# A four-layer kernel: distances of one batch made among the softmax tiles of another in the last attention, two slots for the row norms, split loads in the first feed-forward

## What is computed

```python
    x = x + _layernorm(_L3_attn_ref(_layernorm(x, axis=-1), ...), axis=-1)
```

```python
        scores = jnp.einsum('bid,bjd->bij', q, k) / jnp.sqrt(...)
        qp = _linear(hidden_states, Wtq, btq)
        diff = qp[:, :, None, :] - qp[:, None, :, :]
        dist_sq = jnp.sum(diff * diff, axis=-1)
        phase_diff = jnp.arctan2(diff[..., 1], diff[..., 0])
        forward_bias = 0.5 * (1.0 + jnp.cos(phase_diff))
        mean_dist = jnp.mean(dist_sq, axis=(-1, -2), keepdims=True)
        std_dist = jnp.std(dist_sq, axis=(-1, -2), keepdims=True, ddof=1)
        threshold = mean_dist + THRESHOLD_FACTOR * std_dist
        valid = (dist_sq <= threshold) & causal[None]
        masked = jnp.where(binary_attn == 0, -jnp.inf, scores)
        weights = jax.nn.softmax(masked, axis=-1)
        context = jnp.einsum('bij,bjd->bid', weights, v)
        output = _linear(context, Wo, bo)
        quantum_output = _linear(r_embed, Wfq, bfq)
        return hidden_states + output + 0.1 * quantum_output
```

## Time and profile before

| | us |
|---|---|
| three runs, median (lowest, highest) | 2629.41 (2624.09, 2635.16) |
| the profiled execution | 2632.55 |
| its span | 2630.6 |
| PE busy in it | 1926.2 |
| DVE busy in it | 1713.3 |

### The profile page before, as it was taken

One profiled execution on the slowest core, in us unless ns is written; L12 is line 12 of the kernel. 1 busy time (PEld: TensorE's weight loads), 2 busy tenths in 40 slices (PEclk: granted clock), 3 DMA queues, 4 the chain that ended last, 5 costly groups with the idle time before them and its releaser, 6 DMA issues. The chain is left out here.

```text
span 2630.6 us, 46533 instructions
## 1 busy us (share of the span) xinstructions
PE 1926.2 (73%) x16472; PEld 1324.4 (50%) x16472; DVE 1713.3 (65%) x4060; ACT 1090.8 (41%) x2021; POOL 847.6 (32%) x627
## 2 busy tenths in 40 slices
PE   4888886387777784559999647787787549995446
PEld 1555554155555553437777524454454338884334
DVE  3777776576555554659999843788888672224564
ACT  1666663254544442204444223555555213331332
POOL 3000000574444421014444334445545169201001
PEclk8999999699999987659999765898988669997667
DMA  3011110210000000010000065566665140000000
...
DMA packets 126467, 145.04 MB, mean 55 GB/s; under 512 B 72472, under 2 KB 100171, under 8 KB 123490
## 3 DMA queue, kind: packets, MB, share of 16 engines
...
## 5 line engine op out<-in xcount | busy, mean ns | idle before, releaser
L407 ACT ACTIVATE l0a_pr<-l0a_sm,l0a_nm 128x512 f32<-128x512 f32 x256 | 184.9, 723 | 147.4 <-DVE l0a_nm L324 146.9
L324 DVE CUSTOM_DVE_ANT_0 l0a_sm<-l0a_ps_s,l0a_tb 128x512 f32<-128x512 f32 x256 | 171.0, 685 | 93.9 <-PE l0a_ps_s L473 90.8
L2606 ACT ACTIVATE l2a_pr<-l2a_ps_s,l2a_nm 128x512 f32<-128x512 f32 x256 | 174.1, 687 | 120.8 <-DVE l2a_nm L2525 119.9
L481 PE MATMUL l0a_ps_p<-top_c_ident,l0a_pr 128*128 128x128 f32 x1024 | 170.4, 290 | 54.2 <-ACT l0a_pT L415 54.1
L481 PEld LDWEIGHTS l0a_ps_p<-top_c_ident,l0a_pr 128*128 128x128 f32 x1024 | 110.0, 143 | 117.1 <-ACT l0a_pr L407 64.7
L2525 DVE TENSOR_REDUCE l2a_nm<-l2a_ps_s 128x2 f32<-128x1024 f32 x128 | 156.7, 1224 | 4.4
L2532 DVE STREAM_TRANSPOSE l2a_tt<-l2a_pr 128x1024 f32<-128x1024 f32 x128 | 158.0, 1234 | 0.1
L1508 POOL TENSOR_TENSOR l1f_h<-l1f_lm,l1f_sg 128x512 f32<-128x512 f32 x72 | 92.6, 1286 | 184.0 <-DVE l1f_lm L1577 184.0
L754 POOL TENSOR_TENSOR l0f_ct<-l0f_raw,l0f_cos_scaled 128x1024 f32<-128x1024 f32 x32 | 76.3, 2386 | 184.1 <-issue 94.7
L1880 ACT ACTIVATE l2f_h<-l2f_ps_h 128x512 f32<-128x512 f32 x128 | 76.7, 599 | 134.7 <-PE l2f_ps_h L1425 128.9
L1635 ACT ACTIVATE l1f_csb<-l1f_ps_c,l1f_b3e 128x512 f32<-128x512 f32 x128 | 88.2, 689 | 104.9 <-PE l1f_ps_c L1425 104.6
...
## 6 DMA issues: line engine op xcount, KB each, us to landing
...
```

The costliest lines, as they stand in the source:

```text
L324: v.tensor_tensor_reduce(sm[j % 4][:, :], ps_s[j % 2][:, :], tb[slot][:, off:off + N][:, ::-1], -1.0, 3e38, ALU.add, ALU.min, nm[:, j % 4: ...
L407: a.activation(pr[j % 4][:, :], sm[j % 4][:, :], ACT.Exp, bias=nm[:, j % 4:j % 4 + 1], scale=-1.0).then_inc(m["p_ready"], 1)
L481: last = pe.transpose(ps_p[j % 2][:, tile(k)], pr[j % 4][:, tile(k)], ident[:, :])
L2606: a.activation(pr[slot][:, 2 * (g % 2) + u, :], ps_s[g % 2][:, u, :], ACT.Exp, bias=nm[:, g % 2, u:u + 1], accum_out=rs[:, n % 2, 2 * (g % ...
```

## The change

1. `RowNorm` moves up and gets a method `pipeline`: statistics of batch b, then normalizing of batch b-1. It takes the place of `LayerNorm` at the start of l0a, l0f, l3a and in the routers of l1f and l2f, with two `zb` buffers; l2a calls the same order through it. (The norms at the start are so in six stages.)
2. The end of l0a runs PE and ACT ahead of DVE with second banks and buffers, and its row norms in two slots, statistics of a batch ahead of the normalizing of the one before.
3. l0f: three semaphores. `tab_loaded` (rotary table, four scales, mask: six transfers), `qkv_loaded` (2), `loaded` (the rest). The tables wait for the first only. PE and ACT no longer wait for `consts_ready` at their start: ACT waits before its first Square, POOL before its first rotation, PE at step 0; all wait for `loaded` at step 0. The order of issue on SP is the same.
4. l3a: loads on three semaphores, order of issue changed so that q, k, v need only nine of them; z turned with two PSUM banks, q and k with two pairs. The phase term with both biases is made for all batches ahead of the loop by four matmuls on `phase` (10 x 512) and added to `z` on DVE (`add_phase`). q is scaled by -SCALE/2^64, so that the mask, times 2^64, is added within the operation that takes the row minimum: `pen` takes one operation, `nmx` none. Context is produced turned (`vt` stationary, `pT` moving), so there is no `cx`, and none of its transposes; the reciprocal of the row sum goes into four operations at the residual. `dist`, `drop`, `xj`, `thr`, `y` have two buffers. DVE's loop runs i from 0 to 4: distances of batch i between the softmax tiles of batch i-1, residual and norm of batch i-2 within it.

The new method, and the two parts of l0f and l0a:

```diff
+    def pipeline(self, v, chain, src, dst, ready, free=None):
+
+        for b in range(B + 1):
+            if b < B:
+                self.statistics(v, chain, b, lambda t: src(b, t))
+            if b:
+                if free is not None and b >= 3:
+                    v.wait_ge(free, b - 2)
+                self.normalize(v, chain, b - 1, lambda t: src(b - 1, t), lambda t: dst(b - 1, t))
+                chain.wait()
+                v.sem_inc(ready, 1)
...
+                for b in range(B + 1):
+                    if b < B:
+                        v.wait_ge(m["y_ps"], b + 1)
+                        ch.link(v.tensor_tensor(y[:, b % 2, :, :], (ps_x, ps_s[0])[b % 2][:, :].rearrange("p (t d) -> p t d", d=D),
+                                                bproj[:, :].unsqueeze(1).broadcast_to([P, NT, D]), ALU.add))
+                        v.sem_inc(m["y_ready"], 1)
+                        ln.statistics(v, ch, B + b, lambda t: y[:, b % 2, t, :])
+                    if b:
+                        ln.normalize(v, ch, B + b - 1, lambda t: y[:, (b - 1) % 2, t, :], lambda t: zb[:, (b - 1) % 2, t, :])
+                        ch.wait()
+                        xb = xs[:, (b - 1) * NT:b * NT, :]
+                        ch.mark(v.tensor_tensor(xb, xb, zb[:, (b - 1) % 2, :, :], ALU.add))
...
                 for l in range(F_DEPTH):
-                    ld(wqkv[:, l, :], w["wqkv"][l])
-                ld(maskf[:, :, :], w["window_mask"])
+                    ld(wqkv[:, l, :], w["wqkv"][l], m["qkv_loaded"])
+                ld(maskf[:, :, :], w["window_mask"], m["tab_loaded"])
...
-                v.wait_ge(m["loaded"], 16 * TOTAL)
+                first.pipeline(v, ch, lambda b, t: xs[:, b * NT + t, :], lambda b, t: r[:, b * NT + t, :], m["r_ready"])
+                v.wait_ge(m["tab_loaded"], 16 * (2 + 2 * F_DEPTH))
```

DVE's loop in l3a and what it calls (`distances`, `variance` and `threshold` hold the operations of L2906 to L2923 with the new buffers), then PE's:

```diff
-                            ch.link(v.scalar_tensor_tensor(out=pen[:, 0:L], in0=dist[:, t, 0:L], scalar=thr[:, 0:1],
-                                                           in1=keep[:, t, 0:L], op0=ALU.is_le, op1=ALU.mult))
-                            ch.link(v.tensor_scalar(pen[:, 0:L], pen[:, 0:L], -1.0, -NEG, ALU.add, ALU.mult))
...
+                def masked(b, t):
+
+                    n, L, u = b * NT + t, (t + 1) * P, t % 2
+                    v.wait_ge(m["drop_ready"], n + 1)
+                    if n >= 2:
+                        v.wait_ge(m["sm_ready"], n - 1)
+                    ch.link(v.scalar_tensor_tensor(out=pen[u][:, 0:L], in0=dist[b % 2][:, t, 0:L], scalar=thr[b % 2][:, 0:1],
+                                                   in1=drop[b % 2][:, t, 0:L], op0=ALU.is_gt, op1=ALU.max))
+                    v.wait_ge(m["s_ps"], n + 1)
+                    if n >= 2:
+                        v.wait_ge(m["p_ready"], n - 1)
+                    v.tensor_tensor_reduce(sm[u][:, 0:L], ps_s[u][:, 0:L], pen[u][:, 0:L], BIG, 3e38, ALU.add, ALU.min,
+                                           nmx[:, n:n + 1]).then_inc(m["sm_ready"], 1)
+
+                def turn(b, t):
+
+                    n, L, u = b * NT + t, (t + 1) * P, t % 2
+                    v.wait_ge(m["pt_ps"], n + 1)
+                    if n >= 2:
+                        v.wait_ge(m["c_ps"], n - 1)
+                    v.tensor_copy(pT[u][:, 0:L], ps_p[:, 0:L]).then_inc(m["pT_ready"], 1)
+                    ch.mark(v.reciprocal(rr[:, n:n + 1], rs[:, n:n + 1]))
+
+                def add_phase(b):
+
+                    zb = z[:, b * NT:(b + 1) * NT, :]
+                    v.wait_ge(m["phase_ps"], b + 1)
+                    v.tensor_tensor(zb, zb, ps_phase[b % 2], ALU.add).then_inc(m["phase_added"], 1)
+
+                def residual(b):
+
                     v.wait_ge(m["y_ps"], b + 1)
-                    ch.link(v.tensor_tensor(y[:, :, :], ps_q[0][:, :].rearrange("p (t d) -> p t d", d=D),
-                                            z[:, b * NT:(b + 1) * NT, :], ALU.add))
+                    v.wait_ge(m["phase_added"], b + 1)
+                    ch.wait()
+                    for t in range(NT):
+                        n = b * NT + t
+                        ch.mark(v.scalar_tensor_tensor(out=y[b % 2][:, t, :], in0=ps_y[:, t, :], scalar=rr[:, n:n + 1],
+                                                       in1=z[:, n, :], op0=ALU.mult, op1=ALU.add))
+                    ch.wait()
                     v.sem_inc(m["y_read"], 1)
-                    ch.link(v.tensor_tensor(y[:, :, :], y[:, :, :], ybias[:, :].unsqueeze(1).broadcast_to([P, NT, D]), ALU.add))
-                    ln.statistics(v, ch, lambda t: y[:, t, :])
-                    ln.normalize(v, ch, lambda t: y[:, t, :], lambda t: yn[:, t, :])
+                    ln.statistics(v, ch, lambda t: y[b % 2][:, t, :])
+
+                def finish(b):
+
+                    ln.normalize(v, ch, lambda t: y[b % 2][:, t, :], lambda t: yn[:, t, :])
                     ch.wait()
                     xb = xs[:, b * NT:(b + 1) * NT, :]
                     ch.link(v.tensor_tensor(xb, xb, yn[:, :, :], ALU.add))
 
+                distances(0, 0)
+                for i in range(B + 1):
+                    for t in range(NT):
+                        if i < B and t:
+                            distances(i, t)
+                        if i == 0 and t:
+                            add_phase(t - 1)
+                        if i:
+                            masked(i - 1, t)
+                            if t == 0 and i >= 2:
+                                residual(i - 2)
+                            if t >= 1:
+                                turn(i - 1, t - 1)
+                            if t == 2 and i >= 2:
+                                finish(i - 2)
+                    if i < B:
+                        variance(i)
+                    if i:
+                        turn(i - 1, NT - 1)
+                    else:
+                        add_phase(NT - 1)
+                    if i + 1 < B:
+                        distances(i + 1, 0)
+                    if i < B:
+                        threshold(i)
+                residual(B - 1)
+                finish(B - 1)
...
+                                scores(b, t + 1)
+                            elif b + 1 < B:
+                                scores(b + 1, 0)
+                            if t == 1 and b + 2 < B:
+                                columns(b + 2)
+                            if t == 3 and b + 1 < B:
+                                totals(b + 1)
...
                             for k in range(t + 1):
-                                last = pe.matmul(context(t), pT[:, t % 2, tile(k)], vt[:, b * NT + k, :], start=(k == 0), stop=(k == t))
+                                last = pe.matmul(ps_v[:, t, :], vt[:, b * NT + k, :], pT[t % 2][:, tile(k)], start=(k == 0), stop=(k == t))
                             last.then_inc(m["c_ps"], 1)
-                    pe.wait_ge(m["cx_ready"], b * NT + NT)
-                    pe.wait_ge(m["reT_ready"], B)
+                    pe.wait_ge(m["cxT_ready"], b + 1)
+                    if b:
+                        pe.wait_ge(m["y_read"], b)
                     for t in range(NT):
-                        last = pe.transpose(ps_t[:, tile(t)], cx[:, t, :], ident[:, :])
-                    last.then_inc(m["ct_ps"], 1)
-                    pe.wait_ge(m["cxT_ready"], b + 1)
-                    for t in range(NT):
-                        pe.matmul(ps_q[0][:, tile(t)], cxT[:, tile(t)], wT[:, 3, :], start=True, stop=False)
-                        last = pe.matmul(ps_q[0][:, tile(t)], reT[:, tile(b * NT + t)], wfqT[:, :], start=False, stop=True)
+                        last = pe.matmul(ps_y[:, t, :], cxT[:, tile(t)], wT[:, 3, :], start=True, stop=True)
                     last.then_inc(m["y_ps"], 1)
```

589 lines of the change are left out of this document (305 added, 284 removed).

## The result

The changed kernel takes 2536.32 us, median of four runs (2533.08 to 2537.45), against 2629.04 us before in the same session (2624.09 to 2635.16): ratio 0.9644, 95% interval 0.9622 to 0.9667. The forecast was 2539 us, with a range of 2521 to 2563. Beside two later kernels the changed kernel was run and profiled a second time (after_again): 2539.28 us, ratio 0.9659 (0.9641 to 0.9677).

What follows compares the result with a forecast made beforehand. No single engine was taken as the bound: hand-overs within a batch and at stage starts cost waits. Gains 4.8 + 3.4 + 16.3 + 4.5 + 2.5 + 59.4 = 90.9 us gave 2541.7, as median 2539, range 2521 to 2563.

Steps and rivals of the forecast that it cites:

- l3a, the start: Start of l3a: first distance 9.5 us earlier, as projections wait for nine loads and no longer for all four norms.
- l3a, the rounds: Loop of l3a: a round of 20.9 us where batches stood 36.42 apart; the whole stage gains 59.4, bounds 45 and 65.
- The one wait that the prediction left: In l3a's rounds DVE waits 1.5 us before the residual for the output of batch i-1.
- l0f: Start of l0f: two-slot norms and split loads bring the first Square from 489.58 to 473.3, gain 16.3, bounds 16.5 and 5.
- q and k are made meanwhile, as PE and ACT wait for neither: Start of l0f: q and k are made while DVE makes the tables, from about 469.8 to 473.3.
- l0a, start: Start of l0a: two slots save DVE some 4.5 us; the matmul at 29.69 comes at 24.9, gain 4.8, bounds 2 and 5.
- l0a, end: End of l0a: four waits for POOL, 4.5 us in sum, go except the last; gain 3.4, bounds 2.9 and 3.8.
- the rival with the wide fall: Untouched PE-bound stages: granted clock falls from 0.849 to 0.81, costing 93 us, slower than before above that; chance 0.02.
- l2f: Router of l2f: third and fourth norm both lie beside POOL's fold at 5.39 us each; gain 2.5, bounds 0 and 9.
- the rival's result: In l2f the norms get ahead of the fold and the gain is 9 us, total 2532; chance 0.05.
- PE did not become the bound: Rival for l3a: PE at clock 0.5 makes a round take 24.5 us instead of 20.9, total 2553; chance 0.14.
- The rounds of 30 us: Rival for l3a: ACT or PE stands in line for the other batch's item, rounds of 30, total 2566; chance 0.05.

Runs made afterwards that it cites:

- norms_serial: The changed kernel with each batch normalized right after its own statistics, in all stages sharing the helper and at l0a's end; 2550.63 us, ratio 0.9705.
- qkv_first: The changed kernel with l0f's first-layer q, k, v weights loaded ahead of everything else and waited for alone; 2531.76 us, ratio 0.9627.
- cx_late: The changed kernel with l3a's residual behind the second distance and ACT's context copy behind the squares, in rounds 2 and 3; 2533.28 us, ratio 0.965.
- l3a_serial: The changed kernel with l3a's batches one after another again, the same operations in another order; 2562.76 us, ratio 0.9743, l3a 159.39 us.
- l3a_only: The kernel before with the new l3_attn alone; 2565.71 us, ratio 0.9757, l3a 132.81 us.
- resid_late: The changed kernel with l3a's residual behind the second distance in rounds 2 and 3, and the last but one behind a masked tile; 2541.69 us, ratio 0.966.
- rest_only: The changed kernel with the old l3_attn; 2595.71 us, ratio 0.9871, l3a 193.32 us.
- l0f_whole: The changed kernel with l0f's tables, ACT and first q waiting again for every load of the stage; 2548.95 us, ratio 0.9706.
- fold_late: The changed kernel with POOL's fold in l2f started only when the last router tile has been split into its parts; 2516.88 us, ratio 0.9577.
- both: The changed kernel with the edits of fold_late and cx_late together; 2521.45 us, ratio 0.9596.

## Why the prediction was right, step by step

- **l3a, the start** (9.5, bounds 5 to 13.6). 13.3 in the profile after, 9.9 in after_again. The same code takes 34.0 to 39.3 us here, and the waits for the v projection differ with it (10.8 us in sum in norms_serial, 12.9 after, 16.1 in after_again). The length follows PE's granted clock 14 to 34 us into the stage. These windows are qkv_first (start 34.05), after (35.85) and after_again (39.31); cx_late stands between, with 0.87 and 37.04, and in all eleven profiles of this start a higher clock there goes with a shorter start. The step held; it has a spread that one profile doesn't show.

```profile
2361.97:2381.97 20.00, 15.48 (x103) 12.12 (x103) 8.75 (x38) 7.96 (x13) 4.05 (x4) 1.00 0.00 1
```

```profile
2360.40:2380.40 20.00, 16.09 (x94) 11.84 (x92) 8.74 (x38) 6.31 (x11) 4.05 (x4) 0.91 0.00 1
```

```profile
2366.82:2386.82 20.00, 16.31 (x70) 11.37 (x69) 7.66 (x35) 5.29 (x8) 3.86 (x4) 0.74 0.00 1
```

- **l3a, the rounds.** Round 0 forecast 13.5, measured 13.57. Round 1 forecast 15, measured 16.1 and 16.4. Rounds 2 and 3 forecast 41.8, measured 41.3 and 39.2. The tail forecast 23.4, measured 23.7 and 23.4. The one wait that the prediction left, before the residual, is where it said, at 0.9 to 2.7 us in round 2 and 1.7 to 2.0 in round 3 against 1.5, and 3 us in the tail. The terms that the prediction gives for it, 6.0 less about 1 and 1.7, leave 3.3 and not 3.5 to 3.9; l3a_serial, where nothing covers this chain, shows 3.0.
- **l0f** (16.3). 14.7 and 15.4 at the first Square, 15.8 and 15.2 on the stage. The step that failed in part: "q and k are made meanwhile, as PE and ACT wait for neither". The first q waited for its weights, and that, not the tables, set the Square; qkv_first showed that with the weights first it is the tables again. Its Square comes 1.4 earlier than in the first profile. A second reading was off too. The sum over the windows tells how much has moved in all, not that the first 2.3 MB are the first to be complete. In the profile after, 2.2 MB had moved by 454 and 3.0 by 456, yet the mask, the last of those 2.3 MB, was there only at 456.1. So the tables did wait for a transfer, 0.99 and 0.53 us, which the prediction had named as a sign of being wrong; it is small here, and it is gone in qkv_first.
- **l0a, start** (4.8): 4.9. The cause was only partly the named one, as norms_serial showed (1.7 for the order, 3.2 for the wait on the transposes that is gone).
- **l0a, end** (3.4): 4.8. The step said that the last of four waits for POOL stays. It doesn't: the third batch's normalization stands between the last statistics and the last normalization, and covers POOL's power. From the first output to the last residual it is 16.03 us, against 20.82.
- **l0a, between**, forecast 0. From the first transposes of the weights (PE, `l0a_pr`) to the first output on DVE it was 373.8 us and is 369.1 in both profiles, 4.7 gained. Windows of 20 us in before and after:

```profile
145.00:165.00 20.00, 16.53 (x167) 10.20 (x170) 14.14 (x45) 12.56 (x21) 0.30 (x1) 0.91 0.14 43
```

```profile
145.00:165.00 20.00, 16.51 (x198) 10.24 (x196) 14.96 (x48) 13.68 (x23) 0.29 (x1) 1.00 0.13 43
```

  Three such falls, some 90 us apart, stand in before and in norms_serial (loops of 373.8 and 373.5); one stands in l3a_only (370.6, with the old l0a), and one each in l3a_serial, qkv_first and resid_late (370.0 to 370.7, with the new l0a); none in after, after_again, rest_only, l0f_whole, fold_late, cx_late and both. Each is worth about 1.5 us. So these 4.7 us can't be put down to the edit: the loop, which no edit touches, takes 370.6 and 373.8 with the old l0a and 368.4 to 373.5 with the new one. The prediction had no step for a clock that changes in code that is not touched, other than the rival with the wide fall; why the falls come and go was not settled.
- **l1f** (4.5): the first gate product on PE comes 4.5 earlier, 12.98 us into the stage against 17.48. The stage is 3.6 shorter.
- **l2a** (0): its norms are where they were. Yet from its start to l2f's first PE work it takes 607.9 us in before and l3a_only, and 609.9 to 613.6 in the others. The last Exp is already 3 us late, so it is lost within the attention loop. norms_serial, which makes l2a's norms one after another, takes 611.1, no more than the changed kernel, so the norms are not the cause; it stays open.
- **l2f** (2.5, bounds 0 to 9): 1.7 in after_again, where two norms met the fold as forecast, and 8.5 in the profile after, where one got ahead of it, which is the rival's result. Which it is depends on when the first transposes run (10.65 and 13.81 us behind PE's start in l2f), so both come in one program. Behind the norm the masks pay as well: 6.0 us beside the fold, 1.6 without it. The prediction priced the norms alone, and the fold's collision is larger than it said: 14 to 20 us, as fold_late shows. The Trainium skill ("SBUF — State Buffer", section "Who interferes with whom") says that when such operations of DVE and GpSimd want the port pair that they share, whoever issues first has it for its whole instruction and the other is blocked; fold_late agrees, with 1.11 against 5.38 for the same norm.

**Sum.** Forecast 90.9; the two spans give 99.3 and 91.6, the medians 92.7. l0a gave some 6 more than forecast, 4.7 of them in the loop that no edit touches, l2a took 3.5 to 4.7, and these nearly cancel. So the total is closer than its terms, and a miss of 3 us on the median (2536 against 2539) is in part luck. Of the rivals, PE did not become the bound: a round is 19.4 to 21.7 us and DVE is busy 81% of the longer one. But PE's clock shows in the wait before the residual: in round 2 the output products took 2.08 us after and 1.16 in after_again, and the wait was 2.69 and 0.91. The rounds of 30 us came only when the interleaving was undone (29.6).
